# Clearings spread between a group's indirect DMAs in a six-layer decoder kernel, with new orders of work

## What is computed

```python
x = _layernorm(x + _L0_attn_ref(...))    # retention, 8 heads of 16, gated
x = _layernorm(x + _L0_xattn_ref(...))   # cross attention to ctx, masked
x = _layernorm(x + _L0_ffn_ref(...))     # 8 experts, top 2, experts rerouted by a global table
x = _layernorm(x + _L1_attn_ref(...))    # 16 heads of 64
x = _layernorm(x + _L1_xattn_ref(...))   # 16 heads of 8, keys of ctx and x
x = _layernorm(x + _L1_ffn_ref(...))     # attention of 16 heads, norm, 8 experts of 512, top 2, norm
```

## Time and profile before

| | |
|---|---|
| median of 3 runs | 1653.33 us (1649.35 to 1654.88) |
| the profiled execution | 1652.21 us, of which the span is 1650.4 us |
| busy in it | PE 1387.8 us, DVE 1128.9, ACT 937.1, POOL 744.2 |
| mean granted TensorE clock | 0.943 of full speed |
| stages in the span | one 0 to 476 us, two 476 to 1400, three 1400 to 1570, four 1570 to 1650 |

### The profile page before, as it was taken

How to read it: one execution, slowest core, us unless ns; L and a number is a source line. 1 busy time by engine, 2 the same in 40 slices (tenths; PEclk the granted TensorE clock), 3 DMA queues, 4 the chain that set the end, 5 groups by cost and what they waited for, 6 DMA issues and landing times.

```text
span 1650.4 us, 47485 instructions
## 1 busy us (share of the span) xinstructions
PE 1387.8 (84%) x19192; PEld 1120.8 (68%) x19192; DVE 1128.9 (68%) x3503; ACT 937.1 (57%) x2474; POOL 744.2 (45%) x1104
## 2 busy tenths in 40 slices
PE   6899999999968998889988899988899973899900
PEld 5688788787746776666776667766677752798800
DVE  3677777878755767787577876766876774455565
ACT  3455556555524687655877548775568951444411
POOL 5514434325144326556255752447551354354465
PEclk9799999999988999899999999999999996899955
DMA  9932211211120001100010110001000001677543
GB/s 333 385 126 75 76 61 65 71 57 55 36 92 11 15 9 27 33 23 27 9 28 27 32 31 9 25 22 33 26 21 9 18 25 37 215 227 227 171 140 96
DMA packets 112636, 124.07 MB, mean 75 GB/s; under 512 B 22048, under 2 KB 85536, under 8 KB 112160
## 3 DMA queue, kind: packets, MB, share of 16 engines
q1 hardware_dynamic: 105760, 107.26, 20.5%
q0 software_dynamic: 6656, 13.78, 2.5%
HBM read 65.72 MB, written 55.28 MB: 73 GB/s over the span
## 4 chain that ended last, share of the span: by engine, by line
PE 50%; DVE 22%; POOL 10%; ACT 8%; issue 6%; DMA 1%; another core or an unknown queue 1%; SPq 1%; DVEq 0%; POOLq 0%; ACTq 0%
PE bank L1957 5%; PE bank L1824 4%; PE bank L2211 4%; PE bank L2204 4%; PE bank L1809 3%; ACT P L1235 3%; PE bank L2079 3%; POOL rows_x L1085 3%; PE bank L2044 3%; PE bank L1836 3%; DVE P L1589 2%; POOL blank L1012 2%; DVE gs L1588 2%; PE bank L2005 2%; PE bank L1924 2%
## 5 line engine op out<-in xcount | busy, mean ns | idle before, releaser
L1824 PE MATMUL bank<-const,P 128*128 128x128 f32 x1152 | 174.4, 283 | 16.0 <-ACT P L1235 7.2
L1824 PEld LDWEIGHTS bank<-const,P 128*128 128x128 f32 x1152 | 131.2, 144 | 51.7 <-ACT P L1235 16.6
L1235 ACT ACTIVATE P<-bank,gs 128x128 f32<-128x128 f32 x512 | 143.0, 393 | 32.6 <-DVE gs L1578 32.0
L1957 PE MATMUL bank<-XT,wb 128*128 128x256 f32 x512 | 142.4, 399 | 7.7 <-ACT PT L1140 4.3
L1042 POOL TENSOR_TENSOR P<-P,gs 128x512 f32<-128x512 f32 x64 | 66.7, 1049 | 156.3 <-DVE gs L1625 155.8
L1243 ACT ACTIVATE PT<-bank 128x512 f32<-128x512 f32 x192 | 110.6, 616 | 35.5 <-PE bank L1824 35.0
L1588 DVE TENSOR_REDUCE gs<-bank 128x8 f32<-128x512 f32 x128 | 87.4, 683 | 50.6 <-PE bank L1809 33.0
L1095 POOL DMA_INDIRECT y_rows<-R,gidx x80 | 76.8, 960 | 96.8 <-DVE R L1764 82.7
L1578 DVE TENSOR_REDUCE gs<-bank 128x4 f32<-128x512 f32 x128 | 83.2, 685 | 44.1 <-PE bank L2079 43.7
L1957 PEld LDWEIGHTS bank<-XT,wb 128*128 128x128 f32 x512 | 88.2, 192 | 24.9 <-ACT PT L1140 8.6
L1336 ACT ACTIVATE PT<-bank,Q 128x256 f32<-128x256 f32 x160 | 66.3, 476 | 60.0 <-PE bank L2204 53.1
(11 more groups left out here) (286 smaller groups left out, 3818.7 us busy)
## 6 DMA issues: line engine op xcount, KB each, us to landing
Q<-in_wm SPq DMA_DIRECT2D x40, 578.5 KB
rows_x<-blank SPq DMA_DIRECT2D x4, 5016.0 KB, 37.7
y_mid<-PT SPq DMA_DIRECT2D x16, 512.0 KB, 3.0
y_mid<-D SPq DMA_DIRECT2D x16, 512.0 KB, 2.8
XW<-rows_x SPq DMA_DIRECT2D x40, 132.0 KB
wb<-in_wb SPq DMA_DIRECT2D x1, 4228.0 KB, 15.7
V<-in_ctxT SPq DMA_DIRECT2D x32, 128.0 KB, 2.5
P<-y_rows SPq DMA_DIRECT2D x32, 128.0 KB, 2.3
```

What stands on the lines that cost most here:

```text
L1235: ins = act.activation(P[s][:, i, 128 * g:128 * g + 128], banks[s][i][:, 128 * g:128 * g + 128], ACT.Exp, bias=gs[s][:, 0, 4 * i + g:4 * i ...
L1824: last = pe.transpose(tile(banks[s][i], t), tile(P[s][:, i, :], t), ident)
L1957: mm(half(s, 2 * (e % 2) + k), tile(B("gu"), 2 * e + k), XT[s][:, :], start=True, stop=True).then_inc(a_up_ps.of(s), 1)
```

## The change

In `fetch` and in the scatter one clearing stands between any two of the four indirect DMAs, three in all, where before four stood between the second and the third. The tables of orders are made anew, except `sp1`, `pool3` and `sp4`. For the rest each engine has the same steps with the same instructions, in another order.

```diff
             def clear_again():
-                for _ in range(4):
-                    pool2(pool, pool.memset(blank[:, :], 0.0))
+                pool2(pool, pool.memset(blank[:, :], 0.0))
...
                 for t in range(T):
-                    if t:
-                        clear_again()
                     for k in range(2):
+                        if t or k:
+                            clear_again()
                         pool.indirect_dma_start(y_two[s][:, k, 128 * t:128 * t + 128], None, d[f"y_mid{n * SLOTS + s}"][:, :], bass.IndirectOffsetOnAxis(
...
                 for t in range(T):
-                    if t:
-                        clear_again()
                     for k in range(2):
+                        if t or k:
+                            clear_again()
                         pool.indirect_dma_start(d["rows_x"][:, :], bass.IndirectOffsetOnAxis(
...
-    pool1=(0, 2, 1, 1, 0, 2, 1, 1, 2, 2, 3, 2, 0, 1, 1, 2, 0, 1, 2, 1, 1, 1, 2, 1, 3, 1, 1, 1, 3, 1, 2, 2, 0, 1, 3, 2,
+    pool1=(0, 3, 1, 1, 0, 1, 1, 1, 2, 2, 3, 2, 0, 1, 1, 1, 0, 1, 1, 1, 2, 1, 1, 1, 2, 1, 3, 2, 1, 1, 2, 2, 0, 1, 3, 2,
...
-    pe1=(0, 8, 1, 2, 2, 4, 1, 2, 3, 2, 2, 1, 3, 2, 0, 1, 1, 1, 3, 1, 1, 1, 0, 1, 1, 2, 2, 1, 3, 1, 2, 1, 0, 1, 2, 1,
+    pe1=(0, 5, 1, 1, 0, 3, 2, 1, 1, 1, 3, 1, 2, 3, 3, 1, 1, 1, 3, 1, 1, 1, 3, 1, 2, 1, 1, 1, 0, 1, 3, 1, 1, 1, 0, 1,
...
-    sp3=(3, 1, 0, 2, 1, 1, 2, 1, 1, 1, 2, 1, 3, 1, 4, 1, 5, 1, 6, 1, 4, 1, 5, 1, 7, 1, 6, 1, 8, 1, 7, 1, 9, 1, 8, 1,
+    sp3=(2, 1, 0, 1, 1, 1, 3, 1, 0, 1, 1, 1, 2, 1, 3, 1, 4, 1, 5, 1, 6, 1, 4, 1, 5, 1, 6, 1, 7, 1, 8, 1, 7, 1, 9, 1,
```

More of the change, by code:

```diff
@@ L136 @@
            3, 14, 2, 15, 2, 12, 1, 13, 1, 14, 2, 13, 1, 15, 2, 14, 1, 13, 1, 15, 1, 14, 1, 15, 1, 14, 1, 15, 1, 16, 1,
[3 rows of a table removed]
[3 rows of a table added]
            19, 3, 18, 2, 20, 2, 21, 2, 18, 1, 22, 1, 19, 2, 22, 1, 20, 2, 19, 1, 23, 2, 20, 2, 21, 2, 22, 2, 21, 1,
[8 rows of a table removed]
-    act1=(0, 4, 1, 3, 2, 2, 0, 1, 2, 1, 3, 3, 1, 1, 0, 3, 2, 1, 0, 1, 1, 1, 0, 1, 3, 1, 1, 1, 0, 2, 2, 1, 1, 1, 0, 1,
[64 rows of a table removed]
-    dve1=(0, 7, 1, 1, 2, 2, 0, 1, 1, 1, 0, 1, 3, 2, 1, 3, 0, 1, 2, 1, 1, 1, 3, 1, 1, 1, 2, 2, 3, 2, 0, 1, 1, 1, 2, 1,
[17 rows of a table removed]
[8 rows of a table added]
+    act1=(0, 4, 1, 3, 0, 1, 2, 3, 3, 3, 1, 1, 0, 3, 2, 1, 0, 1, 1, 1, 0, 1, 1, 1, 3, 1, 0, 2, 1, 1, 2, 1, 0, 1, 1, 2,
[65 rows of a table added]
+    dve1=(0, 7, 1, 1, 2, 2, 0, 1, 1, 1, 0, 1, 3, 2, 1, 3, 0, 1, 2, 1, 1, 1, 3, 1, 1, 1, 2, 2, 3, 2, 0, 1, 1, 1, 2, 1,
[17 rows of a table added]
           15, 1, 13, 1, 12, 1, 14, 2, 15, 1, 12, 1, 14, 2, 13, 1, 15, 1, 13, 1, 15, 1, 13, 1, 14, 2, 15, 1, 13, 1, 14,
           1, 13, 1, 15, 1, 13, 1, 14, 2, 13, 1, 14, 2, 13, 1, 15, 1, 14, 1, 15, 1, 13, 1, 14, 2, 15, 1, 14, 1, 13, 1,
[37 rows of a table removed]
-    pe1=(0, 8, 1, 2, 2, 4, 1, 2, 3, 2, 2, 1, 3, 2, 0, 1, 1, 1, 3, 1, 1, 1, 0, 1, 1, 2, 2, 1, 3, 1, 2, 1, 0, 1, 2, 1,
[87 rows of a table removed]
-    sp3=(3, 1, 0, 2, 1, 1, 2, 1, 1, 1, 2, 1, 3, 1, 4, 1, 5, 1, 6, 1, 4, 1, 5, 1, 7, 1, 6, 1, 8, 1, 7, 1, 9, 1, 8, 1,
[4 rows of a table removed]
[37 rows of a table added]
+    pe1=(0, 5, 1, 1, 0, 3, 2, 1, 1, 1, 3, 1, 2, 3, 3, 1, 1, 1, 3, 1, 1, 1, 3, 1, 2, 1, 1, 1, 0, 1, 3, 1, 1, 1, 0, 1,
[87 rows of a table added]
+    sp3=(2, 1, 0, 1, 1, 1, 3, 1, 0, 1, 1, 1, 2, 1, 3, 1, 4, 1, 5, 1, 6, 1, 4, 1, 5, 1, 6, 1, 7, 1, 8, 1, 7, 1, 9, 1,
[4 rows of a table added]
     pool3=(0, 1, 1, 1, 2, 1, 3, 1, 4, 1, 5, 1, 6, 1, 7, 1, 8, 1, 9, 1, 10, 1, 11, 1, 12, 1, 13, 1, 14, 1, 15, 1, 16,
@@ L366 @@
            32, 1, 33, 1, 34, 1, 35, 1, 36, 1, 37, 1, 38, 1, 39, 1),
-    act3=(0, 2, 1, 1, 0, 3, 2, 1, 1, 4, 3, 1, 2, 4, 3, 1, 4, 1, 3, 3, 5, 1, 4, 4, 6, 1, 5, 2, 8, 1, 5, 2, 7, 1, 6, 4,
[6 rows of a table removed]
-    dve3=(0, 1, 1, 1, 2, 1, 0, 1, 3, 1, 1, 1, 2, 1, 4, 1, 5, 1, 3, 1, 4, 1, 6, 1, 7, 1, 5, 1, 6, 1, 8, 1, 7, 1, 9, 1,
[4 rows of a table removed]
-    pe3=(3, 1, 0, 4, 2, 1, 1, 1, 0, 1, 1, 3, 0, 1, 1, 1, 0, 1, 2, 1, 1, 1, 2, 3, 3, 1, 1, 1, 3, 1, 2, 1, 3, 1, 5, 1,
[13 rows of a table removed]
+    act3=(2, 1, 0, 1, 1, 1, 0, 1, 1, 1, 0, 3, 1, 3, 3, 1, 2, 4, 4, 1, 3, 4, 5, 1, 4, 4, 6, 1, 5, 4, 7, 1, 6, 1, 8, 1,
[6 rows of a table added]
+    dve3=(0, 1, 1, 1, 2, 1, 0, 1, 1, 1, 2, 1, 4, 1, 3, 1, 5, 1, 3, 1, 4, 1, 6, 1, 7, 1, 5, 1, 6, 1, 8, 1, 9, 1, 7, 1,
[4 rows of a table added]
+    pe3=(3, 1, 2, 1, 0, 1, 1, 1, 0, 4, 1, 4, 2, 3, 0, 2, 2, 1, 1, 1, 3, 2, 2, 1, 4, 1, 3, 1, 1, 1, 2, 1, 4, 1, 3, 1,
[14 rows of a table added]
     sp4=(0, 1, 1, 1, 0, 1, 2, 1, 1, 1, 3, 1, 0, 1, 1, 1, 4, 1, 5, 1, 2, 1, 3, 1, 4, 1, 2, 1, 3, 1, 4, 1, 6, 1, 7, 1,
@@ L395 @@
          11, 1, 12, 1, 15, 1, 13, 1, 14, 1),
-    pool4=(0, 1, 1, 1, 0, 1, 2, 1, 3, 1, 0, 1, 2, 1, 1, 1, 4, 1, 2, 1, 1, 1, 3, 1, 5, 1, 4, 1, 6, 1, 3, 1, 4, 1, 5, 1,
-           6, 1, 7, 1, 8, 1, 6, 1, 7, 1, 10, 1, 5, 1, 8, 1, 9, 1, 7, 1, 11, 1, 8, 1, 10, 1, 12, 1, 9, 1, 11, 1, 9, 1,
-           11, 1, 13, 1, 10, 1, 14, 1, 15, 1, 13, 1, 14, 1, 15, 1, 12, 1, 13, 1, 15, 1, 12, 1, 14, 1),
-    act4=(0, 1, 1, 1, 2, 1, 3, 1, 4, 1, 5, 1, 6, 1, 7, 1, 8, 1, 9, 1, 10, 1, 11, 1, 13, 1, 12, 1, 15, 1, 14, 1),
-    dve4=(0, 2, 1, 1, 2, 2, 1, 1, 3, 1, 4, 1, 3, 1, 4, 1, 5, 1, 6, 2, 7, 1, 5, 1, 7, 1, 8, 2, 10, 1, 11, 1, 9, 2, 11,
-          1, 12, 1, 10, 1, 13, 1, 14, 1, 15, 1, 13, 1, 15, 1, 12, 1, 14, 1))
+    pool4=(0, 1, 1, 1, 0, 1, 3, 1, 2, 1, 0, 1, 2, 1, 1, 1, 4, 1, 2, 1, 3, 1, 1, 1, 5, 1, 6, 1, 3, 1, 4, 1, 6, 1, 7, 1,
+           5, 1, 4, 1, 8, 1, 7, 1, 5, 1, 9, 1, 6, 1, 10, 1, 8, 1, 7, 1, 11, 1, 8, 1, 9, 1, 12, 1, 10, 1, 11, 1, 9, 1,
+           11, 1, 13, 1, 10, 1, 14, 1, 13, 1, 15, 1, 12, 1, 14, 1, 15, 1, 13, 1, 15, 1, 12, 1, 14, 1),
+    act4=(0, 1, 1, 1, 2, 1, 3, 1, 4, 1, 6, 1, 5, 1, 7, 1, 8, 1, 9, 1, 10, 1, 11, 1, 13, 1, 12, 1, 15, 1, 14, 1),
+    dve4=(0, 2, 2, 1, 1, 1, 2, 1, 3, 1, 1, 1, 3, 1, 4, 1, 6, 1, 5, 1, 4, 1, 7, 1, 5, 1, 6, 1, 7, 1, 8, 2, 10, 1, 9, 1,
+          11, 1, 9, 1, 10, 1, 11, 1, 12, 1, 13, 1, 14, 1, 13, 1, 15, 2, 12, 1, 14, 1))
 A_PE = (("qk_ps", 4), ("vg_ps", 2), ("st_ps", 2), ("y_ps", 1), ("h_ps", 1), ("o_ps", 1), ("kv_ps", 2), ("x_ps", 1),
```

## The result

The changed kernel takes 1634.1 us (median of five runs, 1626.85 to 1637.31) beside 1653.33 us (1649.35 to 1657.1): a ratio of 0.9875, 95% interval 0.9857 to 0.9893.

A forecast was written before the change was run, and what follows sets the result against it. TensorE was taken to bound stage one and stage two's body, POOL being busiest at stage two's start. -2.2 - 2.9 - 1.5 + 0.7 = -5.9 us, from 1653.33 to 1647.4 us, range 1638 to 1655.

The forecast's parts named there:

- One group: POOL's four indirect DMAs with their clearings: 7.02 us becomes 6.29, 0.73 less, the DMAs no dearer.
- Start of stage two: The first slot's norm root waits behind fetches on POOL; with three fetches shorter, 2.2 us less.
- Turns: Where passes change in stage two, slot 0's four scatters delay a norm: 4 x 0.73 = 2.9 us less.
- Other groups: Seven further groups on the chain in stage two: nothing taken, bounds nothing and 5.1 us.
- End of stage two: The last two scatters, for which the third stage's loads wait: 2 x 0.73 = 1.5 us less.
- New orders of stages one and two: Steps moved in the engines' orders, mostly by one or two places: nothing, plus or minus 4 us.
- The rival in which they hold TensorE up: TensorE's new order blocks ready steps, about 30 new waits of 0.45 us: 1661 us in all, chance 0.15.
- Third stage: SP loads rows of four tiles before the first weights, so the stage starts 0.7 us later in effect.
- Stage four: A few of POOL's and VectorE's steps move: nothing, plus or minus 1 us.
- VectorE beside a clearing: VectorE's norm instructions overlapping clearings: fewer clearings give less than 0.5 us, nothing in the sum.
- Rival 1: All 16 groups on the chain pay 0.73 us each, 11.7 less: 1642.3 us in all, chance 0.20.
- The sign of being wrong: TensorE's idle in either body, stage one or two, moving over 5 us would mean orders decide, not clearings.

The follow-up runs named there:

- e9: Kernel before with one clearing between any two DMAs of a group, all orders old, a second run: 1628.9 us, ratio 0.9865.
- e1: Kernel before with one clearing between any two DMAs of a group, all orders old: 1629.0 us, ratio 0.9872.
- e15: Kernel before with one clearing between any two DMAs, all orders old, run again in another set: 1614.1 us, ratio 0.9877.
- e2: Kernel after with four clearings back in the middle of each group, all orders new: 1649.3 us, ratio 1.0001.
- e7: Kernel before with three clearings in the middle of each group instead of four, orders old: 1615.5 us, ratio 0.9902.
- e16: Kernel before with two clearings in the middle of each group instead of four, orders old: 1602.8 us, ratio 0.9805.
- e8: Kernel before with no clearings inside the groups, orders old: 1585.9 us, ratio 0.9724.
- e11: Kernel before with two clearings between any two DMAs of a group, orders old: 1673.6 us, ratio 1.0137.
- e5: Kernel before with one clearing between DMAs only in the 16 groups on its chain, orders old: 1619.1 us, ratio 0.9919.
- e12: Kernel before without clearings in the groups, new orders of stages one, two and four: 1672.2 us, ratio 1.0123.
- e14: Kernel before without clearings in the groups, new orders of stages one, two and four, another set: 1585.6 us, ratio 0.97.

## Why the prediction was wrong

- **One group** (0.73 us shorter, DMAs no dearer): right, 6.36 us for the one shown, 0.72 less in the median, and 955 ns.
- **Start of stage two**, -2.2: 6.4 measured. The first gap gave its 1.5; the clock, which didn't fall a second time, and a fourth group behind it were not in the sum.
- **Turns**, -2.9: mis-sized, and here the prediction failed. I counted one group in each of four turns, the scatter of slot 0, because TensorE waits visibly behind it. There are three turns, each with seven or eight groups, and they gave 7.0, 3.3 and 4.8 us (8.3, 5.2 and 5.6 in the second profile of the same kernel, e9). Slot 0's fourth scatter stands in the last stretch. More than half of the 15.1 us is TensorE's own busy time, which the sum had nowhere.
- **Other groups**, nothing: the step that failed with it. The reason given was that TensorE is busy 725.21 of 800 us and POOL less than half. Both are averages over turns and quiet stretches. Cut apart, the quiet stretches are TensorE's and the turns are POOL's, and 23 of the 32 groups stand in the turns, 8 at the start and in the last stretch.
- **End of stage two**, -1.5: right for the pair. Its first scatter stands 14.57 us before SP's first load in e1 (1361.54 and 1376.11) instead of 16.0, and 14.5 to 14.6 in e9, e15 and the kernel after. The whole last stretch, with two scatters more, gave only 1.05 us in e1 and nothing in e9.
- **New orders of stages one and two**, nothing within 4: -9 in stage one, and in stage two -1 to +2 in the first set (+6 and -11 between single profiles of later ones). The rival in which they hold TensorE up did not come about in the first two stages; in the third something like it did.
- **Third stage**, +0.7: +11, by orders that I had not priced. **Stage four**, nothing within 1: -3.4. The misses of the orders cancel, so e2 is at 1.0001, and the whole error of the forecast is stage two. That they cancel is luck.
- **VectorE beside a clearing**, under 0.5 us in favour: the other way. With the same orders VectorE is busy 655.72 us instead of 652.34 over the nine stretches. It is the places, not the number: with four, three, two and no clearings in the middle it is 652.3, 652.9, 651.2 and 649.6 us (before, e7, e16, e8), with three or six between the DMAs 654.4 to 656.2 (e1, e9, e15, e11). So fewer clearings do give VectorE a little, and spreading them costs more than that; why, was not tested. The rule of the Trainium skill's page "SBUF — State Buffer", section "Who interferes with whom", would have given a gain for fewer clearings too: these rows agree in direction, and show nothing for or against it on their places.
- **Rival 1**, 11.7 us less for every group on the chain: nearest, with the 16 groups worth 13.2 in e5. Its limit was to take the chain for a list: the other 16 groups gave 2.4 by themselves, and all 32 gave 20.
- **The sign of being wrong** (TensorE's idle time in a body moved by over 5 us, "for then the orders decide"): it was a bad sign. In e1, with all orders old, TensorE's idle time between the start and the last stretch fell from 74.4 to 68.0 us, by the places alone.

## What to carry to other kernels

Before a busy share is taken as cover, cut the stretch where the work changes: POOL, busy 46% over 800 us, set the pace in some 460 of them and had little to do in the rest. When several pipelined slots pass through one engine in a written order, price a cut there at nearly its full length for all of them, not for those on the drawn chain alone. And judge new orders stage by stage: here +11, -9, -3.4 and up to +2 added to nothing that a total could show.

## What the runs showed of the hardware

The same kernel (e12, e14) was 1.2% slower than the kernel before in one set and 3.0% faster in another. Of the 83 us between its second stages some 37 are TensorE's waits without a visible releaser, and 45 are the same matmuls taking longer at a granted clock of 0.93 instead of 0.97. In the one sort of sets these waits grew as GpSimd's indirect DMAs stood closer (8.2, 12 to 15, 17 to 21, 42.9 us). In the other they stayed at 2.2 to 6.2 us at any spacing, and the kernel before itself was 15 to 19 us faster there. What makes the two sorts is not known. So a form with closer DMAs should be run on several occasions before it is taken.
